# Two weight loads of an MoE kernel padded to 96 and 112 rows

## The chip, the cores and the metric

The kernel runs on one core of a Trainium2 chip. Times are device microseconds (us). The core has a matrix engine (PE, TensorE), a vector engine (DVE), a scalar engine (ACT), a general engine (POOL, GpSimd) and a queue engine (SP) that here only issues transfers and waits. Sixteen DMA engines move data between the chip's main memory (DRAM) and the on-chip memory of 128 partitions (rows). Rows named PEld are weight loads of PE, and rows named SPq are what SP's sequencer does.

## The reference

The input x is 16 x 256 tokens of 128 numbers. The result is x plus an attention term plus a feed-forward term, both computed from the layer-normed tokens:

```
xn = layernorm(x)
q, k, v = xn (16 heads of 8) @ Wq.T, Wk.T, Wv.T
probs = softmax over c of (q . k of the same token) / sqrt(128)
attn  = probs * (v summed over the 256 tokens of each c)
cw    = the 2 largest of softmax(xn @ gate_w + gate_b), of 16 experts
y     = sum over the 2 experts of cw * ((silu(xn@w1+b1) * (xn@w3+b3)) @ w2 + b2)      (inner width 176)
z     = (silu(xn@sw1+sb1) * (xn@sw3+sb3)) @ sw2 + sb2                                 (inner width 352)
out   = x + attn + y + z
```

## The kernel before

Each engine has its own program, written out by hand, and they meet through semaphores. There are 4096 tokens in 32 tiles of 128, and 8 groups of 4 tiles. The work goes through these stages.

1. Norm, transposes and gate logits of all groups (PE lines 766 and 773), then the choice of two experts for each token and of a slot in a sorted list of 79 tiles of 128 slots (DVE, up to line 513).
2. The scatter: POOL issues 64 indirect transfers (line 384), each of which writes 128 token rows into the DRAM list `xslot`. The first 32 (first expert) run while the rest of stage 1 and stage 3 run, the other 32 (second expert) after them.
3. The dense part z: `up` (PE lines 793 and 794), `gates` on ACT (line 700), `gated_up` on DVE (line 529) and `down` (PE line 814). DVE adds its result to X (`add_z`, line 535). DVE also does the attention term, `attend` (lines 544 and 549), which multiplies the softmax by `Vb`, the summed v of all 16 c on all partitions. `attend` of groups 0 to 3 stands ahead of the loop over groups 4 to 7 in DVE's program, so `gated_up` of group 4 comes behind it, and PE's `up` waits for `gated_up`, since it writes the same banks.
4. The slot loop: for each of the 79 slot tiles PE transposes the tokens (line 890), multiplies by the expert's w1 and w3 (lines 894 and 897), transposes the product (lines 906 and 907) and multiplies by w2 (line 916). POOL scatters the result into `ydram` (line 392). PE passes four semaphores (lines 868 to 871) before it: w13 split, w2 landed, the list of experts, and the dense part's products.
5. The sum of both experts' results and X (lines 644 and 646), and the store.

SP is one queue in order. Behind the loads of inputs and the fill of `xslot` it issues the load of w13 (line 290), the load of w2 (line 291), the store of the 16 x 128 sums `vS` into `vdram` (line 294), and, once that has landed and all slots are indexed, the broadcast load of `Vb` from `vdram` (line 297). Then it waits for all 64 scatters (line 301) and issues the loads of slot tiles, 72 KB each, 12 in flight (line 307).

`w2` is 89 rows: 88 of weights (half of the inner width of 176) and one of the bias. The third chunk of `sw2` is 97 rows: 96 of weights and one of the bias. The products read `w2[0:89]`, `w2[0:88]` and `sw2[0:97]` (lines 814 and 916).

Of the kernel before, what the change touches and what calls it, by code (L numbers as in the profile page):

```python
# [23 lines left out]
P = 128  # L24
# [10 lines left out]
H, D = 16, 8  # L35
NE, F = 16, 176
FH = F // 2
F2 = 2 * F
SF = 352
SCH = [(0, 128), (128, 128), (256, 96)]  # L40
# [15 lines left out]
BIG = 3.0e38  # L56
WQ = NE * F2 // NW
NBIAS = NE * F2

# [35 lines left out]
def build(nc, d):  # L95
    ctx = ExitStack()
    with ctx:
        def sb(name, shape, dt=F32):
            return ctx.enter_context(nc.sbuf_tensor(name, shape, dt))

        def sem(name):
            return ctx.enter_context(nc.semaphore(name))
# [26 lines left out]
        sw1 = sb("sw1", [P, SF])  # L129
        sw3 = sb("sw3", [P, SF])  # L130
        sw2 = sb("sw2", [P, NB, P])
        sbc = sb("sbc", [P, NB, 2])

        fw = sb("fw", [P, NE * (F2 + 2 * P)])
        fz = fw[:, 0:FZ * ROW]
        w13 = fw[:, 0:NE * F2]
        w2 = fw[0:FH + 1, NE * F2:NE * (F2 + 2 * P)]
        braw = sb("braw", [P, NBIAS // P])
        bres = sb("bres", [P, NBIAS // P])
        bprt = sb("bprt", [P, 3, NBIAS // P], BF16)  # L140

        w13h = sb("w13h", [P, NE * F2], F32R)
        w13l = sb("w13l", [P, NE * F2], F32R)
# [26 lines left out]
        def landing(c):  # L170

            flat, n = (XR[:].rearrange("p t r -> p (t r)"), c) if c < YX else (xnT, c - YX)
            return flat[:, n * 2 * CL * P:(n + 1) * 2 * CL * P].rearrange("p (t k e) -> p t k e", k=2, e=P)
# [6 lines left out]
        yb = Wk[:, 0:UN * P].rearrange("p (u e) -> p u e", e=P)  # L180
        raT = Wk[0:FH + 1, UN * P:(UN + 4) * P].rearrange("p (b w) -> p b w", b=2)

# [17 lines left out]
        l_kc, l_gate, l_ws, l_sh, l_w13, l_w2, l_b = (sem(n) for n in ("l_kc", "l_gate", "l_ws", "l_sh", "l_w13", "l_w2", "l_b"))  # L200
# [48 lines left out]
        def has(j, fixed):  # L249
            return not fixed or 0 <= j < NS  # L250
# [4 lines left out]
        @block.sync  # L255
        def _(sp):
            def load_x(g):
                two = slice(g * QT, (g + 1) * QT)
                four = slice(g * QT // CL, (g + 1) * QT // CL)
                sp.dma_start(X[:, two, :].rearrange("p (c b) e -> p c (b e)", b=CL), x_v[:, four, :]).then_inc(l_x[g], 16)  # L260

            load_x(0)
            sp.dma_start(kc[:], d["kc"]).then_inc(l_kc, 16)
            sp.dma_start(gw[:], d["gate_w"]).then_inc(l_gate, 16)
            sp.dma_start(gb[:], d["gate_b"].to_broadcast([P, NE])).then_inc(l_gate, 16)
            load_x(1)
            sp.dma_start(wbd[:].rearrange("p a b -> p (a b)"), d["wqk"]).then_inc(l_ws, 16)
            load_x(2)
            load_x(3)
            sp.dma_start(sw1[:], d["sw1"]).then_inc(l_sh, 16)  # L270
            sp.dma_start(sw3[:], d["sw3"]).then_inc(l_sh, 16)
            sp.dma_start(sw2[:, 0:2, :], d["sw2"][0:256, :].rearrange("(c p) n -> p c n", p=P)).then_inc(l_sh, 16)
            sp.dma_start(sw2[0:97, 2, :], d["sw2"][256:SF + 1, :]).then_inc(l_sh, 16)
            sp.dma_start(sbc[:, 0:2, :], d["sb_a"]).then_inc(l_sh, 16)
            sp.dma_start(sbc[0:96, 2:3, :], d["sb_b"]).then_inc(l_sh, 16)
            sp.dma_start(braw[:], d["biases"]).then_inc(l_b, 16)
            sp.wait_ge(k_fz, 2)
            for j in range(0, NS, FZ):
                n = min(FZ, NS - j)
                sp.dma_start(xs_v[j:j + n].rearrange("s p r -> p s r"),  # L280
                             fz.rearrange("p (q r) -> p q r", r=ROW)[:, 0:n, :]).then_inc(d_fill, 16)

            sp.wait_ge(k_bprt, 1)
            for k in range(3):
                sp.dma_start(bdram[k].rearrange("(p w) -> p w", p=P), bprt[:, k, :]).then_inc(d_bst, 16)
            sp.wait_ge(d_bst, 48)
            sp.wait_ge(k_xz, 1)
            sp.dma_start(bsp[0:3, :], bdram[:, :]).then_inc(d_bup, 16)
            sp.wait_ge(d_fill, 16 * NF)
            sp.dma_start(w13, d["w13"]).then_inc(l_w13, 16)  # L290
            sp.dma_start(w2, d["w2"]).then_inc(l_w2, 16)

            sp.wait_ge(s_vs, 1)
            sp.dma_start(vdram.rearrange("a (c e) -> (a c) e", c=C), vS[:]).then_inc(d_vs, 16)
            sp.wait_ge(d_vs, 16)
            sp.wait_ge(s_idx, 4)
            sp.dma_start(Vb.rearrange("p c e -> p (c e)"), vdram.to_broadcast([P, C * P])).then_inc(d_vb, 16)

            for k in range(2):
                for h in range(2):  # L300
                    sp.wait_ge(d_sc[k][h], 16 * (NT // 2))

            def load(j, u, used):

                if used is not None:
                    sp.wait_ge(d_y[u], 16 * used)
                sp.dma_start(RX[:, u, :], xs_v[j]).then_inc(d_rx[u], 16)

            sp.wait_ge(s_wl, NW)
            for u in range(UN):  # L310
                load(u, u, None)
            with sp.Fori(1, NS // UN) as it:
                for u in range(UN):
                    load(it * UN + u, u, it)
            for j in range(NS - NS % UN, NS):
                load(j, j % UN, j // UN)

            for u in range(UN):
                sp.wait_ge(d_y[u], 16 * ((NS - u + UN - 1) // UN))

            for c in range(NC):
                sp.dma_start(landing(c), y_v[:, c * CL:(c + 1) * CL, :, :]).then_inc(d_yl[c], 16)  # L322
            sp.wait_ge(d_o, 16 * NC)
# [326 lines left out]
        def _(act):  # L650
# [80 lines left out]
            def run(j, u, fixed):  # L731
# [10 lines left out]
                if has(j - 1, fixed):  # L742
                    b = (u - 1) % 2
                    act.wait_ge(r_at, j)
                    act.wait_ge(r_dn, max(j - 2, 0) if fixed else j - 2)
                    act.activation(raT[0:FH, b, :], PS[0:FH, 4 + b, 0:2 * P], ACT.Copy).then_inc(r_att, 1)  # L746

# [8 lines left out]
        def _(pe):  # L756
# [129 lines left out]
            def run(j, u, fixed):  # L886
# [14 lines left out]
                if has(j - 1, fixed):  # L901
                    b = (u - 1) % 2
                    pe.wait_ge(r_a, j)
                    if fixed and j == 1:
                        pe.wait_ge(s_za, NG)
                    pe.transpose(PS[0:FH, 4 + b, 0:P], ra[:, b, 0:FH], ident)  # L906
                    pe.transpose(PS[0:FH, 4 + b, P:2 * P], ra[:, b, FH:F], ident).then_inc(r_at, 1)  # L907
                if has(j - 2, fixed):
# [5 lines left out]
                    for k in range(2):  # L914
                        n = FH + 1 - k
                        ins = pe.matmul(PS[:, 6 + b, 0:P], raT[0:n, b, k * P:(k + 1) * P],  # L916
# [8 lines left out]
def constants():  # L925
    import numpy as np
    k = np.zeros((P, KW), np.float32)
    i, j = np.arange(P)[:, None], np.arange(P)[None, :]
    k[:, K_ID:K_ID + P] = i == j
    k[:, K_BLK:K_BLK + P] = i // D == j // D  # L930
    k[:, K_U:K_U + P] = -1.0 * (i >= j)
    k[:, K_ONE:K_ONE + P] = 1
    k[:, K_REV:K_REV + NE] = NE - np.arange(NE)
    k[:, K_TILE:K_TILE + NS] = np.arange(NS)
    kb = k.view(np.int32)
    kb[:, K_TOK:K_TOK + NT] = (i * NT + np.arange(NT)[None, :]) * 2
    kb[:, K_TOK2:K_TOK2 + NT] = kb[:, K_TOK:K_TOK + NT] + 1
    kb[:, K_PAD:K_PAD + FZ] = 2 * N + np.arange(FZ)[None, :] * P + i
    return k


def arrays_of(inp):

    import numpy as np
    a = {n: np.asarray(v) for n, v in inp.items()}
    f = "L0_ffn_"
    w13 = np.concatenate([a[f + "w1"], a[f + "w3"]], axis=2)
    b13 = np.concatenate([a[f + "b1"], a[f + "b3"]], axis=1)
    w2 = np.zeros((FH + 1, NE, 2, P), np.float32)
    w2[0:FH] = a[f + "w2"].reshape(NE, 2, FH, P).transpose(2, 0, 1, 3)  # L950
    w2[FH, :, 0] = a[f + "b2"]
    r = {
        "x": a["L0_attn_x"].reshape(N, P),
        "kc": constants(),
        "wqk": np.concatenate([np.tile(a["L0_attn_Wq"], (H, H)), np.tile(a["L0_attn_Wk"], (H, H)),
                               np.tile(a["L0_attn_Wv"].T, (H, H))], axis=1),
        "gate_w": a[f + "gate_w"], "gate_b": a[f + "gate_b"].reshape(1, NE),
        "biases": b13.reshape(P, NBIAS // P),
        "sw1": a[f + "sw1"], "sw3": a[f + "sw3"], "sw2": np.concatenate([a[f + "sw2"], a[f + "sb2"].reshape(1, P)], axis=0),
        "sb_a": np.stack([a[f + "sb1"][:256].reshape(2, P).T, a[f + "sb3"][:256].reshape(2, P).T], axis=2),  # L960
        "sb_b": np.stack([a[f + "sb1"][256:], a[f + "sb3"][256:]], axis=1)[:, None, :],
        "w13": w13.transpose(1, 0, 2).reshape(P, NE * F2),
        "w2": w2.reshape(FH + 1, NE * 2 * P),
    }
    return {n: np.ascontiguousarray(v) for n, v in r.items()}

# [17 lines left out]
```

## Time and profile before

| | us |
|---|---|
| median of 3 runs | 291.55 |
| lowest, highest | 291.29, 292.16 |
| the profiled execution | 292.58 |
| its span | 290.8 |
| PE busy | 217.7 (75%) |
| DVE busy | 188.0 (65%) |
| POOL busy | 156.6 (54%) |
| ACT busy | 115.0 (40%) |

The span is divided into 40 slices of 7.3 us in the profile's second part. Its digits are tenths of each slice:

```profile
PE   0679959599499000599989999999999999995000
DVE  4998885498969105446476666666666666662386
ACT  2134246930043100032316666666565665662000
POOL 6323005777788777772003666666666666666000
PEclk9999998689799655599999999999999999999555
DMA  6999591222111124112300333333333333311698
```

The line PEclk is the TensorE clock that was granted (9: full, 5: half). Three slices hold a PE at 0 in the middle of the kernel, from about 94 to 116 us. POOL alone works there. The slot loop is the long stretch from the 21st slice on.

### The profile page before, as it was taken

The numbers are of one execution on the slowest core, as the hardware profiler recorded it, in microseconds if no ns is written. First come the engines' busy times: TensorE is split into PE (matmuls) and PEld (weight loads), VectorE is DVE, ScalarE is ACT, GpSimd is POOL, SyncE is SP. The second block draws the span as 40 slices with busy tenths as digits, with TensorE's granted clock in tenths as the row PEclk, the third lists the DMA queues.
The fourth block names the chain that finished last, engine by engine and source line by source line (L and its number), as shares of the span: only waits on it lengthen the run. The fifth ranks groups of instructions, "written<-read, shape, count | busy, mean of one in ns | idle before, by whom it ended". The sixth has DMA issues, their size and how long they took to land.

```text
span 290.8 us, 5484 instructions
## 1 busy us (share of the span) xinstructions
PE 217.7 (75%) x1323; PEld 177.7 (61%) x1325; DVE 188.0 (65%) x518; ACT 115.0 (40%) x329; POOL 156.6 (54%) x170
## 2 busy tenths in 40 slices
PE   0679959599499000599989999999999999995000
PEld 0569723597147000257389999999898998994000
DVE  4998885498969105446476666666666666662386
ACT  2134246930043100032316666666565665662000
POOL 6323005777788777772003666666666666666000
PEclk9999998689799655599999999999999999999555
DMA  6999591222111124112300333333333333311698
GB/s 187 314 304 300 148 378 77 86 74 85 75 66 65 74 101 170 61 63 77 75 0 26 101 100 104 91 104 96 88 103 99 93 96 95 96 55 47 203 365 308
DMA packets 35394, 36.74 MB, mean 126 GB/s; under 512 B 5493, under 2 KB 30566, under 8 KB 35030
## 3 DMA queue, kind: packets, MB, share of 16 engines
q1 hardware_dynamic: 28498, 24.54, 28.4%
q0 software_dynamic: 4576, 9.91, 10.1%
q10 hardware_dynamic: 2304, 2.10, 2.1%
q8 instruction: 7, 0.11, 0.2%
q14 instruction: 9, 0.07, 0.1%
HBM read 18.67 MB, written 17.86 MB: 126 GB/s over the span
## 4 chain that ended last, share of the span: by engine, by line
PE 58%; another core or an unknown queue 15%; DVE 11%; DMA 7%; ACT 3%; SPq 3%; issue 1%; POOL 0%; POOLq 0%; DVEq 0%
PE PS L897 13%; PE PS L916 12%; PE PS L894 4%; PE PS L773 4%; PE PS L793 4%; PE PS L814 4%; PE PS L906 3%; PE PS L794 3%; DMA xnT<-ydram 3%; PE PS L890 3%; PE PS L907 3%; SPq L322 3%; DMA gate<-vdram 2%; DVE st L405 2%; PE PS L766 2%
## 5 line engine op out<-in xcount | busy, mean ns | idle before, releaser
L392 POOL DMA_INDIRECT ydram<-fw x79 | 75.9, 960 | 59.1 <-issue 33.3
L384 POOL DMA_INDIRECT xslot<-XR,idx x64 | 68.1, 1064 | 39.8 <-DVE idx L513 20.6
L916 PE MATMUL PS<-fw 89*128 (+1 forms) x316 | 48.7, 276 | 0.1
L629 DVE TENSOR_TENSOR prod<-prod,PS 128x176 f32<-128x176 f32 x79 | 26.7, 338 | 32.2 <-ACT prod L741 32.2
L793 PE MATMUL PS<-xnT,sw 128*128 (+3 forms) x36 | 21.8, 690 | 28.3 <-DVE sS L529 28.3
L916 PEld LDWEIGHTS PS<-fw 89*128 89x128 f32 (+1 forms) x316 | 41.4, 190 | 0.7 <-issue 0.3
L741 ACT ACTIVATE prod<-PS 128x176 f32<-128x176 f32 x79 | 25.1, 318 | 29.8 <-PE PS L897 29.5
L700 ACT ACTIVATE sS<-PS,sbc 128x512 f32<-128x512 f32 (+1 forms) x18 | 12.2, 686 | 61.8 <-PE PS L794 61.7
L897 PE MATMUL PS<-w13h,rxh 128*128 x79 | 34.9, 442 | 0.8 <-DVE rxl L624 0.8
L746 ACT ACTIVATE fw<-PS 88x256 f32<-88x256 f32 x79 | 30.0, 380 | 0.9 <-PE PS L907 0.6
L793 PEld LDWEIGHTS PS<-xnT,sw 128*128 128x128 f32 (+1 forms) x36 | 6.3, 202 | 38.3 <-DVE sS L529 33.8
L736 ACT ACTIVATE rxh<-PS 128x128 fp32r<-128x128 f32 x79 | 21.9, 278 | 18.6 <-PE PS L890 18.4
L637 DVE TENSOR_SCALAR fw<-PS,fw 128x128 f32<-128x128 f32 x79 | 27.7, 350 | 2.1 <-PE PS L916 1.6
L624 DVE TENSOR_TENSOR rxl<-PS,rxh 128x128 fp32r<-128x128 f32 x79 | 22.9, 291 | 5.0 <-ACT rxh L736 0.3
L897 PE MATMUL PS<-w13l,rxh 128*128 x79 | 25.5, 323 | 0.0
L897 PE MATMUL PS<-w13h,rxl 128*128 x79 | 25.5, 322 | 0.0
L529 DVE SCALAR_TENSOR_TENSOR sS<-PS,sbc,sS 128x512 f32<-128x512 f32 (+1 forms) x18 | 13.4, 747 | 17.4 <-ACT sS L700 17.1
L894 PE MATMUL PS<-bsp,sel 128*128 x79 | 24.5, 310 | 0.0
L814 PEld LDWEIGHTS PS<-sw,sS 128*128 128x128 f32 (+1 forms) x192 | 23.2, 199 | 1.5 <-issue 1.5
L814 PE MATMUL PS<-sw,sS 128*128 128x128 f32 (+1 forms) x192 | 23.3, 282 | 0.0
L906 PE MATMUL PS<-kc,prod 128*88 128x128 f32 x79 | 21.6, 274 | 0.1
L890 PE MATMUL PS<-kc,fw 128*128 128x128 f32 x79 | 21.5, 274 | 0.0
(123 smaller groups left out, 372.0 us busy)
## 6 DMA issues: line engine op xcount, KB each, us to landing
fw<-xslot SPq DMA_DIRECT2D x79, 72.0 KB, 1.9
xslot<-fw SPq DMA_DIRECT2D x6, 864.0 KB, 8.8
fw<-in_w SPq DMA_DIRECT2D x1, 2816.0 KB, 9.5
X<-in_x SPq DMA_DIRECT2D x4, 512.0 KB, 6.2
XR<-ydram SPq DMA_DIRECT2D x8, 256.0 KB, 5.5
xnT<-ydram SPq DMA_DIRECT2D x8, 256.0 KB, 8.0
out<-X ACTq DMA_DIRECT2D x16, 128.0 KB, 5.7
fw<-in_w SPq DMA_DIRECT2D x1, 1424.0 KB
```

What stands on the lines that cost most here:

```text
L384: pool.indirect_dma_start(xslot, bass.IndirectOffsetOnAxis(ap=idx[:, k, t:t + 1], axis=0), XR[:, t, :], None).then_inc(d_sc[k][h], 16)
L392: pool.indirect_dma_start(ydram, bass.IndirectOffsetOnAxis(ap=RX[:, v, P:P + 1].bitcast(I32), axis=0), yb[:, v, :], None).then_inc(d_y[v], 16)
L629: dve.tensor_tensor(ra[:, b, :], sg[:, b, :], PS[:, 2 + b, F:F2], ALU.mult).then_inc(r_a, 1)
L637: dve.tensor_scalar(yb[:, v, :], PS[:, 6 + b, 0:P], RX[:, v, P + 1:P + 2], None, ALU.mult).then_inc(r_y, 1)
L746: act.activation(raT[0:FH, b, :], PS[0:FH, 4 + b, 0:2 * P], ACT.Copy).then_inc(r_att, 1)
L793: pe.matmul(PS[0:m, k, :], sw1[:, f:f + m], xv, start=True, stop=True)
L814: ins = pe.matmul(zt, sS[0:k, b, c, t * P:(t + 1) * P], sw2[0:k, c, :], start=(c == 0), stop=(c == NB - 1))
L890: pe.transpose(PS[:, b, 0:P], RX[:, v, 0:P], ident).then_inc(r_tp, 1)
L894: pe.matmul(PS[:, 2 + b, 0:F2], sel[:], bsp[:, bass.ds(e * F2, F2)], start=True, stop=False)
L897: ins = pe.matmul(PS[:, 2 + b, 0:F2], x[:, b, :], w[:, bass.ds(e * F2, F2)], start=False, stop=(k == 2))
L906: pe.transpose(PS[0:FH, 4 + b, 0:P], ra[:, b, 0:FH], ident)
L916: ins = pe.matmul(PS[:, 6 + b, 0:P], raT[0:n, b, k * P:(k + 1) * P], w2[0:n, bass.ds(e * 2 * P + k * P, P)], start=(k == 0), stop=(k == 1))
```

## The change

Both tensors get rows of zeros in DRAM and their loads bring them along: `w2` from 89 to 96 rows of 16 KB, the third chunk of `sw2` from 97 to 112 rows of 512 bytes. The products read the same rows as before. No instruction of any engine is added, removed or moved; only the shapes of two transfers change. Lines of the kernel after are 2 higher than those of the kernel before.

```
+FP = 96
+SP3 = 112
...
-        w2 = fw[0:FH + 1, NE * F2:NE * (F2 + 2 * P)]
+        w2 = fw[0:FP, NE * F2:NE * (F2 + 2 * P)]
...
-            sp.dma_start(sw2[0:97, 2, :], d["sw2"][256:SF + 1, :]).then_inc(l_sh, 16)
+            sp.dma_start(sw2[0:SP3, 2, :], d["sw2"][256:256 + SP3, :]).then_inc(l_sh, 16)
...
-    w2 = np.zeros((FH + 1, NE, 2, P), np.float32)
+    w2 = np.zeros((FP, NE, 2, P), np.float32)
     w2[0:FH] = a[f + "w2"].reshape(NE, 2, FH, P).transpose(2, 0, 1, 3)
     w2[FH, :, 0] = a[f + "b2"]
+    sw2 = np.zeros((256 + SP3, P), np.float32)
+    sw2[0:SF] = a[f + "sw2"]
+    sw2[SF] = a[f + "sb2"]
```

## Rows read from the trace of the kernel before

**Rows 1.** Chain that ended last, in order of time: start us, us, what.

```profile
63.13 44.19 another core or an unknown queue
```

**Rows 2.** Timeline of DVE; in brackets the idle time before and its releaser.

```profile
62.89 0.20 DVE L513 CAST idx<-sm 128x16 int32<-128x16 f32 x1
87.53 2.48 DVE L582 TENSOR_TENSOR w13l<-fw,w13h 128x704 fp32r<-128x704 f32 x3
95.03 0.70 DVE L605 TENSOR_TENSOR PS<-pr,se 128x512 f32<-128x512 f32 x1
112.24 0.76 DVE L544 TENSOR_TENSOR PS<-PS,gate 128x256 f32<-128x256 f32 x2 [16.51 <-DMA gate<-vdram]
```

**Rows 3.** Timeline of PE.

```profile
93.88 1.02 PE L794 MATMUL PS<-xnT,sw 128*128 x2
119.36 2.02 PE L793 MATMUL PS<-xnT,sw 128*96 x2 [24.46 <-DVE sS L529]
150.34 0.38 PE L890 MATMUL PS<-kc,fw 128*128 128x128 f32 x2
```

**Rows 4.** DMA issues: transfer, queue, count, KB each, median us from issue to landing.

```profile
fw<-xslot SPq DMA_DIRECT2D x79, 72.0 KB, 1.9
fw<-in_w SPq DMA_DIRECT2D x1, 2816.0 KB, 9.5
fw<-in_w SPq DMA_DIRECT2D x1, 1424.0 KB
gate<-vdram SPq DMA_DIRECT2D x1, 1024.0 KB, 4.8
sw<-in_sw SPq DMA_DIRECT2D x1, 48.5 KB
vdram<-vS SPq DMA_DIRECT2D x1, 8.0 KB, 67.6
```

**Rows 5.** Timeline of SP's queue: start us, us, line, transfer, count.

```profile
35.90 0.33 SPq L290 DMA_DIRECT2D fw<-in_w  x1
36.27 0.29 SPq L291 DMA_DIRECT2D fw<-in_w  x1
39.68 15.91 SPq L294 DMA_DIRECT2D vdram<-vS  x1
107.34 0.34 SPq L297 DMA_DIRECT2D gate<-vdram  x1
134.91 118.95 SPq L307 DMA_DIRECT2D fw<-xslot  x79
```

**Rows 6.** Windows: length; busy of PE, PEld, DVE, ACT, POOL; clock, DMA share, GB/s.

```profile
77.29:91.00 13.71, 13.58 (x62) 8.34 (x63) 10.92 (x16) 4.02 (x5) 11.55 (x7) 0.89 0.16 61
100.00:104.00 4.00, 0.00 (x0) 0.00 (x0) 0.00 (x0) 0.00 (x0) 3.08 (x4) 0.50 0.21 79
112.00:116.00 4.00, 0.00 (x0) 0.00 (x0) 3.62 (x8) 0.00 (x0) 3.12 (x4) 0.50 0.16 57
160.00:258.00 98.00, 98.00 (x754) 92.15 (x753) 64.99 (x205) 60.42 (x206) 65.31 (x69) 1.00 0.35 96
```

**Rows 7.** Timeline of POOL.

```profile
96.86 0.96 POOL L384 DMA_INDIRECT xslot<-XR,idx  x1 [0.30 <-issue]
132.50 0.96 POOL L384 DMA_INDIRECT xslot<-XR,idx  x1 [0.31 <-issue]
```

**Rows 8.** Windows (same columns) around five changes of PE's granted clock.

```profile
38.60:41.60 3.00, 0.00 (x1) 0.03 (x2) 2.78 (x3) 1.36 (x5) 0.00 (x0) 1.00 0.96 413
42.90:46.10 3.20, 3.20 (x5) 1.30 (x4) 2.96 (x10) 1.12 (x2) 0.54 (x1) 0.50 0.33 137
94.90:97.40 2.50, 0.00 (x0) 0.00 (x0) 0.79 (x2) 0.81 (x2) 1.89 (x3) 1.00 0.23 85
119.36:124.70 5.34, 5.34 (x7) 2.08 (x8) 1.35 (x2) 0.68 (x1) 4.02 (x5) 0.50 0.16 55
53.00:59.20 6.20, 5.13 (x24) 5.16 (x25) 2.68 (x5) 6.20 (x11) 4.68 (x6) 0.50 0.23 84
```

More of the change, by code:

```diff
@@ L958, in arrays_of @@
         "biases": b13.reshape(P, NBIAS // P),
-        "sw1": a[f + "sw1"], "sw3": a[f + "sw3"], "sw2": np.concatenate([a[f + "sw2"], a[f + "sb2"].reshape(1, P)], axis=0),
+        "sw1": a[f + "sw1"], "sw3": a[f + "sw3"], "sw2": sw2,
         "sb_a": np.stack([a[f + "sb1"][:256].reshape(2, P).T, a[f + "sb3"][:256].reshape(2, P).T], axis=2),
@@ L962, in arrays_of @@
         "w13": w13.transpose(1, 0, 2).reshape(P, NE * F2),
-        "w2": w2.reshape(FH + 1, NE * 2 * P),
+        "w2": w2.reshape(FP, NE * 2 * P),
     }
```

## The prediction

> **What bounds the kernel now.** I read the chain of work that ended last first. Its longest single piece is no instruction: 44.2 us from 63.13 to 107.34, booked to an unknown queue [rows 1]. What waits at its end is DVE: its last piece of work ends at 95.73, and it then sits idle for 16.5 us until `Vb` (gate<-vdram) has landed, at 112.24 [rows 2]. PE stands behind it: its last `up` ends at 94.90, and the next starts at 119.36, after 24.5 us of idleness that end with DVE's `gated_up` [rows 3].
>
> Why is `Vb` so late? SP's queue says so. It issued the store of `vS` at 39.68, the store landed 67.6 us later, at 107.3, and at 107.34 SP issued the load of `Vb` [rows 4, 5]. The store is 8 KB. What stands right ahead of it in the same queue is the load of w2, issued at 36.27. The load of w13 ahead of that was issued at 35.90 and landed 9.5 us later, at 45.4: 2816 KB in 9.5 us is 296 KB per us. If w2 holds the store from 45.4 to 107.3, its 1424 KB took 61.9 us, or 23 KB per us, a thirteenth of the rate of w13. The 9.5 us hold some fixed time from issue to landing as well (a slot tile of 72 KB needs 1.9 us [rows 4]); with some 1.5 us of that taken off, w13 ran at 350 KB per us, and w2 at a fifteenth. That is one DMA engine of sixteen. The DMA share says the same: 0.21 while w2 was under way and 0.16 when it was done and the same scatters ran on [rows 6]. The difference of 0.05 is about one engine in 16 (0.0625).
>
> The Trainium skill gives the reason, "DMA: Bandwidth & Descriptors", on why a DMA increments its semaphore by 16: the number of engines is the largest one up to 16 that divides the slowest dimensions of both sides. 89 and 97 are primes, so by it these loads had one engine, and 96 and 112 give 16. A rival reading by bytes alone would give w2 some 5 us both before and after, and no change at 291.5 us; the 61.9 us that the queue shows speak for the rule, but no transfer of 96 or 112 rows of any size has a landing time in this trace.
>
> The second thing to see is what waits behind. The slot tiles' loads are issued at 134.91, when the last scatter has landed [rows 5]; POOL issued it at 132.50 [rows 7]. PE enters the slot loop only at 150.34 [rows 3], so now the slots are ready some 13 us before PE is. From there PE is busy all the time (98.0 of 98 us [rows 6]), so the loop's end follows its start.
>
> **The change, part by part.** No engine's instruction moves, so all of it is in the landing times.
>
> *w2.* On all engines it takes 1536 KB / 296 KB per us = 5.2 us after w13, so it has landed by 50.6. Bounds: 1536/350 = 4.4 us, and 66.8 us if it stays where it is (61.9 x 96/89). Nearest is w13, a load of the same kind issued just ahead; I take 5.2. Even 25 us would do for what follows. The 112 KB more are 0.4 us of that, hidden under 12 us of slack. PE's own wait for w2 stands ahead of the slot loop, later than all this.
>
> *The store of `vS`* then lands by about 52. SP next waits for the last slot index, which DVE writes at 63.09 [rows 2], so the load of `Vb` is issued at 63.2 instead of 107.34, and at 4.8 us it has landed by 68. DVE needs it at 95.8: the slack is 27 us. Its 1 MB shares the engines with scatters, as it does now from 107 to 112.
>
> *DVE and PE.* `attend` starts at 95.77 instead of 112.24: 16.5 us earlier. The 7.1 us from there to PE's next `up` stay, so PE restarts at 102.9, after an idle of 8.0 us instead of 24.5. The clock fell 2.5 us after PE stopped at 94.90 and came back 5.3 us after its restart [rows 8]; 8.0 us of idleness are enough for it to fall again, so I take the same slow restart. The dense part ends 16.5 us earlier, at 150.34 - 16.5 = 133.9. With half a clock for 3.2 us only, as after 42.9 [rows 8], it would end 1.1 us sooner; that is worth nothing, because of the next step.
>
> *The slot loop.* PE now comes to it at 133.9 and finds no tile. The new bound is POOL's scatter. It runs at its own pace, 0.96 us and 0.30 us of issue each, with w2 under way (96.86) and without (132.50) [rows 7], and never waits for a transfer; nothing in the change moves it. So the first slot tile is issued at 134.91 as before and lands 1.9 us later, at 136.8, and PE's first transpose starts there instead of at 150.34: a gain of 13.5 us out of the 16.5. The second tile is issued some 0.3 us later (an issue takes that long [rows 5]) and costs perhaps 0.1 us at the start: 13.4.
>
> *The clock at the hand-over.* Between 133.9 and 136.8 PE stands still for 2.9 us. Now it has no such gap there. Two rows bear on it. After a stop of 3.0 us (38.60 to 41.60) the clock still fell, at 42.9, and stayed at 1.2 GHz for 3.2 us with PE busy; another time it stayed there from 53.0 to 59.2 and a bit, 6.2 us [rows 8]. A PE-bound loop loses half of such a stretch: 1.6 us or 3.1 us; nothing is lost if the clock does not fall. The gap is nearest to the first row, so I take 1.6 us and keep 0 and 3.1 for the range.
>
> *sw2, third chunk.* At 23 KB per us its 48.5 KB [rows 4] held one engine for 2.1 us around 10 to 20 us; spread, 0.2 us. Nobody waits for it: PE's first use comes behind the logits of the last group, and DVE's chain up to the indices has no wait for a transfer after the first X. It also lets SP's queue run up to 2 us ahead, so w13 might land at 43.4 rather than 45.4, long before ACT splits it, behind the silus. I take 0; a loss is excluded, since it is 7.5 KB more in a second of 16 engines' shares.
>
> *The sum.* -13.4 + 1.6 = -11.8 us. On the profiled execution of 292.58 us (span 290.8) this gives 280.8; that execution is 1.0 us above the median of the runs, 291.55, so the prediction for the median is 279.75, rounded to 279.8. The tail after the slot loop is the same work, 11.8 us earlier.
>
> **Rivals.**
> *A: the clock stays up at the hand-over.* The gap of 2.9 us is short, and the clock took 2.5 us after the stop at 94.90 to fall [rows 8]. Then -13.4: 278.2 us. Against it: a stop of 3.0 us was enough once.
> *B: the clock stays down for 6 us, or the dense part's restart is slower.* Then -13.4 + 3.1 = -10.3: 281.3 us.
> *C: the load isn't spread, or something else holds the store.* Then `Vb` stays at 107 and the time at 291.5. Against it stand the rate of a fifteenth and the drop of the DMA share.
> *D: slower than before. The scatter is now the bound, and DVE's work on top of it stretches it.* In the trace DVE's subtractions for w13l (8 of them, from 77 us to 90, the last three at 87.53) lie beside seven scatters that keep POOL busy for 11.5 us instead of 7 x 0.96 = 6.7 [rows 2, 6]: 4.8 us more, 0.6 us for each. From 95.8 to 133.9 there would be 40 instructions of DVE (12 `gated_up`, 16 and 8 of `attend`, 4 `add_z`). If each cost POOL 0.6 us, the scatter would end 24 us later and the time be 291.55 - 11.8 + 24 = 303.8; it turns to a loss from 20 such stretches on. Against it: some 24 of the 40 lie over scatters now, from 112 to 133, and all scatters there take 0.96; 3.12 us of POOL in 4 us with DVE at 3.62 is what it has with DVE at 0, 3.08 [rows 6].
> The Trainium skill has the same distinction, "SBUF — State Buffer", on who interferes with whom: a VectorE instruction with two on-chip SBUF inputs contends with GpSimd's reads, one with a single SBUF input does not. The w13l subtraction has two, the 40 have one and PSUM; by that rule D's price would be 0, and the trace agrees with the 0.96 us.
>
> **How the numbers follow.** The forecast (279.8, own range 278.9 to 280.8) has 0.57, A 0.21, B 0.15, C 0.04, D 0.03. The range for 8 in 10 takes in A and B with a little for the run-to-run spread: 277.5 to 282.0. What a measurement can tell from no change is about 0.3%, or 0.9 us. Faster: 0.57 + 0.21 + 0.15 = 0.93. Same: C, 0.04. Slower: D, 0.03.
>
> **What the profile after would show.** SP's wait before the load of `Vb` ends at 63, not 107, and the store of `vS` lands within some 12 us. DVE's wait of 16.5 us is gone and `attend` starts at 95.8. SP's wait for the scatters grows from 27 us to some 67, and the first slot tile is still issued near 134.9. PE's first transpose of the loop is at 136.8, released by a transfer, after 3 to 4 us of idleness, and the granted clock reads 0.5 for some 3 us soon after. The forecast is wrong if the scatters' pace changes (then the loop's start moves with it), if the store still lands beyond 90, or if PE reaches the loop after 137.

## The result and the profile after

The kernel after takes 280.19 us (median of 4 runs, 279.37 to 280.83), the kernel before beside it 291.42 us (median of 4, 290.91 to 292.16): a ratio of 0.961, 95% interval 0.958 to 0.965. The prediction was 279.8 us. The profiled execution took 280.56 us with a span of 278.8, against 292.58 and 290.8 before: 12.0 us less.

SP's queue after, from its timeline (start us, us, line):

```profile
35.44 0.34 SPq L292 DMA_DIRECT2D fw<-in_w  x1
...
40.20 0.33 SPq L296 DMA_DIRECT2D vdram<-vS  x1
60.25 0.34 SPq L299 DMA_DIRECT2D gate<-vdram  x1
134.93 107.50 SPq L309 DMA_DIRECT2D fw<-xslot  x79
```

The load of `Vb` is issued at 60.25 instead of 107.34, and the issue of the store takes SP 0.33 us instead of 15.91 [rows 5]. Why the issue itself took so long stays open; with two engines for w2 (94 rows, below) it takes 0.32 us although the store still lands late. The first slot tile is issued at 134.93, 0.02 us from where it was. The DMA issues (KB each, us to landing) and SP's waits (us in total, times, longest) say why:

```profile
fw<-in_w SPq DMA_DIRECT2D x1, 2816.0 KB, 10.7
fw<-in_w SPq DMA_DIRECT2D x1, 1536.0 KB, 16.4
vdram<-vS SPq DMA_DIRECT2D x1, 8.0 KB, 12.2
gate<-vdram SPq DMA_DIRECT2D x1, 1024.0 KB, 5.6
```

```profile
SPq L303 <- DMA xslot<-XR,idx: 74.2, 1, 74.2
SPq L298 <- DVE idx L515: 19.7, 1, 19.7
```

w2 lands at 52.2 and the store of `vS` at 52.4, not at 107.3 [rows 4]. What releases the load of `Vb` now is the last slot index. DVE's and PE's timelines after:

```profile
89.24 0.70 DVE L607 TENSOR_TENSOR PS<-pr,se 128x512 f32<-128x512 f32 x1
89.97 0.76 DVE L546 TENSOR_TENSOR PS<-PS,gate 128x256 f32<-128x256 f32 x2
```

```profile
97.09 2.02 PE L795 MATMUL PS<-xnT,sw 128*96 x2 [7.98 <-DVE sS L531]
122.46 5.52 PE L816 MATMUL PS<-sw,sS 128*128 128x128 f32 x48
136.83 0.48 PE L892 MATMUL PS<-kc,fw 128*128 128x128 f32 x1 [8.85 <-DMA fw<-xslot]
```

`attend` follows its predecessor without a wait; the 16.5 us of [rows 2] are gone. PE's stop before group 4 is 8.0 us instead of 24.5 [rows 3]. Then, in the last row, comes the new wait: PE ends the dense part at 127.98 and stands still for 8.9 us until the first slot tile lands. The chain that ended last (in order of time, from 128 us on) runs through POOL up to that point:

```profile
131.24 0.95 POOL xslot L386
132.49 2.27 DMA xslot<-XR,idx
135.33 2.36 DMA fw<-xslot
```

The windows after (columns as in [rows 6]) show the two ends of the account:

```profile
42.90:46.10 3.20, 3.20 (x9) 1.43 (x8) 2.96 (x10) 1.74 (x3) 0.60 (x1) 1.00 1.10 317
53.00:59.20 6.20, 6.20 (x58) 6.20 (x58) 5.60 (x11) 6.15 (x10) 4.68 (x6) 1.00 0.14 48
128.00:132.80 4.80, 0.00 (x0) 0.00 (x0) 0.69 (x1) 0.00 (x0) 3.58 (x5) 0.99 0.15 53
132.80:143.05 10.25, 5.79 (x22) 4.88 (x23) 1.83 (x7) 2.23 (x9) 0.65 (x1) 0.51 0.46 98
```

In the first two the clock is at its full level where it was at half before [rows 8]. A third such stretch was near 78 us: the PE row that starts at 77.42 before takes 2.02 us, the same two matmuls at 73.06 after take 1.10. Together they brought the dense part forward by 5.8 us more than the change did, and it was worth nothing, since PE only waited longer. In the last one it is at half (1.2 GHz), from 132.8 to 143, across the start of the slot loop.

### The profile page after: what moved, and what is told of

It is laid out like the page before. It is cut to its first block, busy times and chain, and to the rows that moved or that the text cites. A ratio compares the mean times of both kernels' runs of the same rounds, so it can differ in the third digit from the quotient of the medians.

```text
span 278.8 us, 5485 instructions
## 1 busy us (share of the span) xinstructions
PE 214.9 (77%) x1324; PEld 176.0 (63%) x1325; DVE 187.9 (67%) x518; ACT 115.0 (41%) x329; POOL 156.2 (56%) x170
## 4 chain that ended last, share of the span: by engine, by line
PE 47%; POOL 25%; DVE 8%; issue 8%; DMA 7%; SPq 3%; ACT 1%; POOLq 0%; DVEq 0%
POOL xslot L386 24%; PE PS L899 14%; PE PS L918 13%; PE PS L896 5%; PE PS L775 4%; PE PS L908 3%; PE PS L892 3%; DMA xnT<-ydram 3%; PE PS L909 3%; SPq L324 3%; DVE st L407 2%; PE PS L768 2%; DVE XR L421 1%; DMA X<-in_x 1%; DMA fw<-xslot 1%
## 5 line engine op out<-in xcount | busy, mean ns | idle before, releaser
L899 PE MATMUL PS<-w13h,rxh 128*128 x79 | 35.7, 452 | 0.0
L795 PE MATMUL PS<-xnT,sw 128*128 (+3 forms) x36 | 20.6, 656 | 11.8 <-DVE sS L531 11.8
L892 PE MATMUL PS<-kc,fw 128*128 128x128 f32 x79 | 22.3, 283 | 9.3 <-DMA fw<-xslot 9.3
L896 PE MATMUL PS<-bsp,sel 128*128 x79 | 25.1, 317 | 0.0
L816 PEld LDWEIGHTS PS<-sw,sS 128*128 128x128 f32 (+1 forms) x192 | 22.1, 191 | 1.5 <-issue 1.5
L816 PE MATMUL PS<-sw,sS 128*128 128x128 f32 (+1 forms) x192 | 22.2, 274 | 0.0
L908 PE MATMUL PS<-kc,prod 128*88 128x128 f32 x79 | 21.9, 277 | 0.1
L909 PE MATMUL PS<-kc,prod 128*88 128x128 f32 x79 | 21.8, 276 | 0.0
## 6 DMA issues: line engine op xcount, KB each, us to landing
fw<-in_w SPq DMA_DIRECT2D x1, 2816.0 KB, 10.7
```

What stands on the lines that cost most here:

```text
L816: ins = pe.matmul(zt, sS[0:k, b, c, t * P:(t + 1) * P], sw2[0:k, c, :], start=(c == 0), stop=(c == NB - 1))
L892: pe.transpose(PS[:, b, 0:P], RX[:, v, 0:P], ident).then_inc(r_tp, 1)
L896: pe.matmul(PS[:, 2 + b, 0:F2], sel[:], bsp[:, bass.ds(e * F2, F2)], start=True, stop=False)
L899: ins = pe.matmul(PS[:, 2 + b, 0:F2], x[:, b, :], w[:, bass.ds(e * F2, F2)], start=False, stop=(k == 2))
```

## The experiments

Nine of the twelve kernels ran on chips on which the kernel before takes 372 to 378 us; three ran on chips on which it takes 291 to 293. What follows keeps the two apart, and the last part of this document says what is seen on the former.

**The load of w2 moved behind the load of `Vb`, still 89 rows** (label k1_w2_late; sw2 unpadded too):

```
-            sp.dma_start(w2, d["w2"]).then_inc(l_w2, 16)
...
             sp.dma_start(Vb..., vdram.to_broadcast([P, C * P])).then_inc(d_vb, 16)
+            sp.dma_start(w2, d["w2"]).then_inc(l_w2, 16)
```

> The kernel before (89 and 97 rows) with the load of w2 issued behind the load of Vb. If the kernel before runs at 291 to 292 beside it: theory (only the place of the slow load in the queue cost time) 279.5 to 281.5, the first slot tile issued at 134.9 and w2 there before PE needs it; rival (a load on one engine costs by itself) 284 or more. If the kernel before runs at 372 or more, only the release times in SP's queue are read.

Measured: 280.90 us (279.65 to 281.86, 4 runs) against 292.72 for the kernel before beside it, ratio 0.960 (0.954 to 0.967). That is the whole gain of the kernel after, without one padded row. SP's queue and two windows of it:

```profile
40.11 0.32 SPq L293 DMA_DIRECT2D vdram<-vS  x1
60.02 0.32 SPq L296 DMA_DIRECT2D gate<-vdram  x1
60.38 0.29 SPq L297 DMA_DIRECT2D fw<-in_w  x1
134.84 107.50 SPq L307 DMA_DIRECT2D fw<-xslot  x79
```

```profile
124.00:128.00 4.00, 3.86 (x35) 3.67 (x33) 3.45 (x9) 0.00 (x0) 3.09 (x4) 1.00 0.21 76
128.00:132.00 4.00, 0.00 (x0) 0.00 (x0) 0.66 (x1) 0.00 (x0) 3.09 (x4) 1.00 0.16 58
```

The DMA share is still 0.21 up to 128 us and then falls to 0.16, the same step as in the kernel before when w2 was through [rows 6]. So w2 still took about 62 us, from some 67 to some 129, and nobody missed it. What cost nearly 12 us was its place ahead of an 8 KB store in one queue, not its length. The scatters, which POOL issues and not SP, were not held in this way beside it: they go out at the same pace, and from issue to landing they take 3.4 us (median) here and in the kernel before, 2.3 us in the kernel after. The kernel also shows that the padding of the sw2 chunk adds nothing that can be measured: it has none of it and reaches the same ratio.

**94 rows, a number between** (e4_rows94, `FP = 94`):

> w2 with 94 rows = 2 x 47, sw2 chunk at 112. By the rule of the largest divisor up to 16 w2 has 2 engines: 1504 KB at 2 x 23 KB per us is 32 us after w13 has landed at about 46, so the store of vS lands at about 78, Vb by 84, ahead of DVE's need at 90 to 96, and the time is that of the kernel after, 279.5 to 281.5. Rival (only the number of bytes or closeness to 96 rows matters): the store lands at 52. Rival (one engine for anything that 16 doesn't divide): the store lands at about 111 and the time is 291 or more.

This ran on a chip on which the kernel before takes 372 us (369.19 against 372.42 us, ratio 0.989, 0.984 to 0.993), so the forecast time can't be judged. SP's queue up to the load of `Vb` can; w13 is issued at 34.95 and lands 9.5 us later:

```profile
40.25 0.32 SPq L296 DMA_DIRECT2D vdram<-vS  x1
77.13 0.34 SPq L299 DMA_DIRECT2D gate<-vdram  x1
```

```profile
58.00:62.00 4.00, 4.00 (x36) 3.82 (x35) 3.12 (x8) 1.14 (x2) 3.08 (x4) 1.00 0.27 101
96.00:100.00 4.00, 0.00 (x0) 0.00 (x0) 0.00 (x0) 0.00 (x0) 2.93 (x4) 0.50 0.16 55
```

The load of `Vb` went out at 77.1; DVE had written the last slot index at 60.0, so what SP waited for from there on is the store, for which 78 had been forecast. From the landing of w13 (34.95 + 9.5 = 44.5) w2 took 32.7 us: 46 KB per us, twice the 23 of one engine. The share while it runs is 0.11 above the share behind it, where one engine gave 0.05. Both rivals are out (the store at 52, the store at 111). That fits the prediction's rule of the largest divisor up to 16 at 89 rows (one engine) and 94 rows (two). At 96 rows the kernel after shows 1536 KB in 6.1 us, 252 KB per us or eleven times the rate of one engine, beside the first scatters: many engines, but the number 16 is not read from it.

**One half of the change alone.** e1_w2_only has 96 rows for w2 and leaves the chunk at 97, e2_sw2_only the other way round:

> Only w2 is padded (96 rows); the third chunk of sw2 stays at 97. Theory (the whole gain is w2, which no longer holds the store of vS in its queue; sw2 is hidden): the time of the kernel after, 280.2 us give or take 0.8; the store of vS lands about 12 us after its issue, the first slot tile is issued at 134.9. Rival (the sw2 chunk carries part of the gain, by letting the queue run 2 us ahead): 281.5 to 282.5.

> Only the third chunk of sw2 is padded (112 rows); w2 stays at 89. Theory: no change to the kernel before, 291.4 us give or take 0.8, with the store of vS still landing at about 107. Rival (sw2 carries part): 289 to 290.

They fell on the same chip: 370.15 and 370.13 us against 372.42, ratios 0.994 (0.988 to 1.000) and 0.993 (0.990 to 0.996). Neither expected time was met, and the two are equal there although one has the long wait and the other not. From SP's queues of the two, in this order:

```profile
40.81 0.32 SPq L296 DMA_DIRECT2D vdram<-vS  x1
61.30 0.34 SPq L299 DMA_DIRECT2D gate<-vdram  x1
159.58 170.43 SPq L309 DMA_DIRECT2D fw<-xslot  x79
```

```profile
39.82 16.63 SPq L296 DMA_DIRECT2D vdram<-vS  x1
107.03 0.34 SPq L299 DMA_DIRECT2D gate<-vdram  x1
158.32 170.74 SPq L309 DMA_DIRECT2D fw<-xslot  x79
```

Padding w2 alone frees the store; padding the chunk alone leaves `Vb` at 107. That much holds. Why no time follows from it there is in the last two rows of each: the slot tiles start at 158 to 160 in both, held by something else. Three more tries with w2 alone (f1_w2_only, h2_w2_only, n1_w2_only) met such chips again, with ratios of 1.007 (1.002 to 1.012), 1.011 (0.991 to 1.030) and 0.994 (0.989 to 0.998). So did three tries of the late w2: 371.41 against 372.42 us (e3_w2_late, no interval; one of its ten executions took 359.07), 1.009 (1.003 to 1.015, f2_w2_late) and 1.004 (0.996 to 1.012, h1_w2_late). The time of w2 alone on a chip at 291 us was not measured; what speaks for all of the gain is k1_w2_late. Two of the expectations:

> The kernel before, 89 and 97 rows, with the load of w2 issued behind the load of Vb instead of ahead of the store of vS. Theory (what cost time was the place of the slow load in the queue, not its length): as the kernel after, 279.5 to 281.5; w2 still takes about 62 us, from about 68 to 130, and is there before the slot loop at 136.8. Rival (a load on few engines costs by itself, by slowing the scatters or the slot tiles): 284 or more.

> w2 with 96 rows, the sw2 chunk left at 97. If the kernel before runs at 291 to 292 beside it: theory (all of the gain is w2) a ratio to it of 0.961 give or take 0.004, some 280.5 us; rival (the sw2 chunk carries part) 0.966 or more. If the kernel before runs at 372 or more: only the issue times in SP's queue are read.

**Is the scatter the new bound?** m1_no_split leaves out the low part of w1 and w3:

```
-                dve.tensor_tensor(w13l[:, cols], w13[:, cols], w13h[:, cols].bitcast(F32), ALU.subtract).then_inc(s_wl, 1)
...
+            for q in range(NW):
+                if q == 0:
+                    act.wait_ge(s_sm, 2 * NB)
+                act.activation(w13l[:, q * WQ:(q + 1) * WQ], w13[:, q * WQ:(q + 1) * WQ], ACT.Copy, scale=0.0).then_inc(s_wl, 1)
```

> The kernel after without DVE's eight subtractions for w13l: ACT writes zeros into w13l in their place, so the low part of w1 and w3 is left out of the products. If the kernel before runs at 291 to 292 beside it: theory (the scatter is the new bound, and the subtractions stretch it by some 5 us) the scatters all take 0.96 us there, the first slot tile is issued near 130 instead of 134.9, and the time falls by 3 to 5 us against the kernel after, to 275.5 to 277.5; rival (the dense part or DVE sets the start of the slot loop) 279.5 or more. If the kernel before runs at 372 or more, only the durations of the scatters are read.

Measured: 274.57 us (273.46 to 276.79) against 291.74 beside it, ratio 0.943 (0.937 to 0.949): 5.6 us less than the kernel after, where 3 to 5 had been forecast. POOL, SP and PE of it:

```profile
82.07 0.96 POOL L386 DMA_INDIRECT xslot<-XR,idx  x1 [0.30 <-issue]
126.82 0.96 POOL L386 DMA_INDIRECT xslot<-XR,idx  x1 [0.30 <-issue]
```

```profile
129.27 106.84 SPq L309 DMA_DIRECT2D fw<-xslot  x79
```

```profile
131.11 0.33 PE L894 MATMUL PS<-kc,fw 128*128 128x128 f32 x1 [1.39 <-DMA fw<-xslot]
```

In the kernel after the scatter at 82 us is this one, and DVE does this beside it:

```profile
82.01 3.05 POOL L386 DMA_INDIRECT xslot<-XR,idx  x1 [0.30 <-issue]
```

```profile
81.74 2.48 DVE L584 TENSOR_TENSOR w13l<-fw,w13h 128x704 fp32r<-128x704 f32 x3
```

Without the subtractions none of those scatters is stretched, the last one goes out 5.7 us earlier, and the first slot tile and PE's first transpose follow by 5.7 us each (131.11 against 136.83). So the scatter is what the kernel after waits for, and a part of the scatter's length is DVE's subtractions. Of the 5.7 us they are some 4.7: six scatters beside them take 10.4 us instead of 5.8. Another 1.1 us is one scatter at 68.09 in the kernel after, stretched to 2.19 us by a DVE instruction (`prod<-kc,se`, 67.98 to 69.44) that m1_no_split has as well; there it meets a scatter only near its end (1.08 us). On the chips at 372 us, where DVE stands still during the scatters, the last one goes out at 126.35 (e1_w2_only), as early as in m1_no_split (126.82).

The rows also tell how much a scatter is stretched. The one at 82.01 ends at 85.06, 0.84 us after DVE's three subtractions end (84.22). The other five beside subtractions, 1.16 to 1.75 us long, and the one at 68.09 end 0.83 to 0.84 us after the DVE instruction that they start with or under, too. So a scatter is held until that instruction is over: the price is what is left of it, not a fixed amount for each. DVE and ACT are also a little less loaded in m1_no_split, but PE ends the dense part at 129.7 there, later than in the kernel after, so the gain isn't from there.

**Does the slow clock at the hand-over cost?** g1_keep_clock is the kernel after with work for PE in the gap:

```
+            for k in (1, 2, 3, 4, 5, 5, 5):
+                pe.wait_ge(k_dm, k)
+                pe.matmul(PS[:, 3, :], sw1[:, 0:P], xnT[:, 0:GW], start=True, stop=True)
...
+                        if k == 1 and t >= NT - 5:
+                            pool.sem_inc(k_dm, 1)
```

> The kernel after with seven matmuls of 0.86 us whose result nobody reads, put on PE between the dense part and the slot loop and released by the last five scatters, so that PE doesn't stand still for 9 us there. If the kernel before runs at 291 beside it: theory (the slow clock at the hand-over costs 1.6 us of the 13.5) 278.3 to 279.5 against 280.2 of the kernel after, with the granted clock at 1.00 from 128 to 143; rival (the start of the loop is bound by the tiles' landings, not by the clock) 280.2 or more; where the dense part ends late, near 134, the matmuls cost up to 3 us. If it runs at 372: no statement on either.

Measured: 279.66 us (278.78 to 280.53) against 292.27 beside it, ratio 0.958 (0.953 to 0.962). Against the 0.961 of the kernel after the intervals overlap, so the timed runs don't tell the two apart. Its windows and PE's timeline, of its fastest execution (278.78 us), do show the mechanism:

```profile
131.45:137.40 5.95, 5.95 (x15) 2.55 (x15) 0.69 (x1) 0.00 (x0) 1.50 (x2) 1.00 0.24 70
137.40:143.00 5.60, 5.03 (x37) 4.24 (x36) 2.75 (x10) 3.14 (x12) 0.06 (x1) 1.00 0.44 111
```

```profile
250.35 1.45 PE L924 MATMUL PS<-fw 89*128 x8
```

The last matmul of the kernel after, and of the kernel before:

```profile
252.69 1.45 PE L918 MATMUL PS<-fw 89*128 x8
```

```profile
264.12 1.45 PE L916 MATMUL PS<-fw 89*128 x8
```

The clock stays at full. From first transpose to last matmul the loop takes 114.5 us in g1_keep_clock, 117.3 in the kernel after and 115.2 in the kernel before. Here the dense part ended late, at 131.45, and the added matmuls pushed the start to 137.30, some 0.7 us after the tile was there (an estimate: issued at 134.73, and 1.9 us to landing). What the slow clock and the late tiles cost the kernel after is thus 2.1 us against before, up to 2.8 against g1. g1 is the fastest complete kernel by its numbers, but not one that is shown to beat the kernel after.

## Why the prediction was right

*w2 on one engine holds the store.* Right. The rate of 23 KB per us, its doubling at 94 rows and the steps of the share fit one engine and two; k1_w2_late shows that the queue's order is the cause.

*w2 lands by 50.6.* 52.2. The store landed at 52.4, not 52. Here w13 took 10.7 us and the 5.2 us for w2 became 6.1, beside the first scatters. The slack covered it.

*`attend` at 95.77, PE again at 102.9, the dense part done at 133.9.* They came at 89.97, 97.09 and 127.98. The links were right (7.1 us from `attend` to `up` in both, a stop of 8.0 us), the anchor was not: I took everything ahead of 95.8 from one execution, in which PE had run at half its clock from 42.9 to 46.1, 53.0 to 59.2 and around 78. In the profiled execution after it did not. Nothing in the change bears on that, and k1_w2_late shows the same full clock in a kernel with the old rows. The error had no price, because the next step takes the later of two times.

*The slot loop starts at 136.8, bound by the scatter.* 136.83; the first tile was issued at 134.93 for 134.91. This is the step that carries the result: the kernel gets 13.5 of the 16.5 us, and in this execution of 22.4.

*+0.1 for the second tile and +1.6 for the clock.* Measured 2.1: the loop is longer than before by that. The second transpose waits 0.42 us for its tile. The clock was at half for 10 us rather than 3: 4 us in the gap, which was 8.9 us and not 2.9, and 6.2 us in the loop. That is the length that rival B had priced at 3.1 us, as if PE were busy throughout. The stretch from the first transpose to the first product with w2, before and after, shows that it isn't:

```profile
150.34:154.37 4.03, 3.24 (x22) 2.52 (x21) 2.22 (x8) 1.81 (x8) 0.00 (x0) 1.00 0.00 0
136.83:142.80 5.97, 5.54 (x20) 4.63 (x21) 1.75 (x6) 2.09 (x8) 0.00 (x0) 0.50 0.63 126
```

It takes 1.9 us more, 0.4 us of waiting for the second tile among them. At full clock PE is idle for 0.8 of the 4.03 us there, while ACT and DVE prepare the first tiles, and a part of the slower matmuls fills that idleness. So the stretch at half clock was twice as long as forecast and a microsecond of it cost about half as much (some 1.5 us for 6.2, an estimate from these rows). That the two errors nearly cancel is luck. Rival A (the clock stays up) did not occur; B's condition did, and its price was too high.

*The sum.* -13.5 + 2.1 is -11.4, and the last matmul ends 11.4 us earlier. The tail behind it is 0.6 us shorter in this execution, which makes the 12.0 of the span. -11.8 was forecast. The medians differ by 11.2.

*sw2 at nothing.* Right as far as k1_w2_late goes.

*SP's wait for the scatters, some 67 us.* 74.2. The prediction's own times give 71.4 (from the issue of the load of `Vb` at 63.2 and 0.3 to 134.9); it counted from the landing of `Vb`, for which SP does not wait. The other 2.9 us are the last slot index, at 60.2 instead of 63.1. Nothing else was built on this number.

*Rivals C and D.* C is out by the landing times. D, DVE's work stretching the scatter: the 40 instructions now lie between 90 and 129, over scatters that all take 0.95 to 0.98 us. The Trainium skill's distinction, "SBUF — State Buffer", on who interferes with whom, by the number of SBUF inputs, agrees with both sides: the subtractions with two such inputs stretch scatters to as much as 3.05 us and their removal ends that, the others don't. D's 0.6 us for each instruction was the mean of the subtractions; m1_no_split's section has what sets it. Two inputs alone are not enough: the instruction at 89.24 above (`PS<-pr,se`, two inputs in SBUF) starts 0.09 us after a scatter, and that scatter takes 0.96 us.

## What to carry to other kernels

Look for a small transfer whose landing takes far longer than its size, and read what stands ahead of it in its queue: here a load of 89 rows ran at the rate of one engine and one of 94 rows at that of two, and an 8 KB store behind it in the same queue waited until it was through. Either give such a load a row count that is a multiple of 16 or put it behind what is urgent; here both gave 4%. When such a wait is removed, the gain ends where the next producer is ready: look for that time (the issue of the first slot tile, 134.9) before promising the whole wait.

## What was not expected of the hardware

On four chips the kernel before took 372 to 378 us, on three others 291 to 293, each beside its own comparisons. The traces there part from the others at 60 to 62 us. A row of PE and a window of e1_w2_only:

```profile
84.34 0.37 PE L783 MATMUL PS<-mbd,xnT 128*128 128x128 f32 x1 [2.42 <-issue]
```

```profile
80.00:98.00 18.00, 2.97 (x8) 2.30 (x8) 0.16 (x1) 0.00 (x0) 13.75 (x16) 0.50 0.16 57
```

PE, which elsewhere does a projection of 16 matmuls in 2 us, stands idle from 80 us on for 1.0 to 2.4 us before each of them, with nothing that it is seen to wait for, and then issues none from 98.7 on; DVE and ACT stop as well. POOL's scatters go on at 0.96 us, and the last one ends at 127.3. DVE starts again at 135.5 and PE at 136.3. The slot loop, in which POOL also scatters, is slower too: PE is busy for 158 of 180 us from 160 on. So from 62 us on PE, DVE and ACT nearly stand still until the last of POOL's 64 scatters is through, and for 8 us more. That is a coincidence in time in these traces, and that the one causes the other is not shown. The cause stays open, and so does the effect of the change on such chips, beyond ratios between 0.989 and 1.011: SP issues the load of `Vb` at 61 instead of 107, but the first slot tile waits for w13's split, which DVE ends some 30 us after the last scatter has landed.
